# The gates of a small mixture of experts: spread by a matmul, or stored and loaded as broadcast rows

## The reference

```python
def _L3_ffn_ref(x, gate_w, gate_bias, w1, w2, w3, ws1, ws2, ws3):
    scores = jax.nn.sigmoid(xf @ gate_w.T)              # 16 experts
    s = scores + gate_bias
    group_scores = s.reshape(T, 4, 4).max(axis=-1)      # keep 2 of 4 groups
    ...
    _, idx = jax.lax.top_k(s_masked, TOPK)              # 4 experts a token
    comb = zeros(T, E).at[arange(T)[:, None], idx].add(scores at idx)
    h = silu(einsum('td,eid->tei', xf, w1)) * einsum('td,eid->tei', xf, w3)   # 64 hidden an expert
    y = einsum('tei,edi,te->td', h, w2, comb)
    z = silu(xf @ ws1.T) * (xf @ ws3.T) @ ws2.T         # the shared expert, no weight
    return x + y + z
```

## Time and profile before

| | us |
|---|---|
| median of 3 runs | 1003.78 |
| lowest, highest | 1000.64, 1007.53 |
| the profiled execution | 1007.03 |
| its span in the trace | 1005.2 |

### The profile page before, as it was taken

How to read it: one execution, slowest core, us unless ns; L and a number is a source line. 1 busy time by engine, 2 the same in 40 slices (tenths; PEclk the granted TensorE clock), 3 DMA queues, 4 the chain that set the end, 5 groups by cost and what they waited for, 6 DMA issues and landing times. The chain is left out here.

```text
span 1005.2 us, 13391 instructions
## 1 busy us (share of the span) xinstructions
PE 730.2 (73%) x3910; PEld 465.9 (46%) x3910; DVE 590.4 (59%) x2022; ACT 355.2 (35%) x634; POOL 251.8 (25%) x304
## 2 busy tenths in 40 slices
PE   2677762849839775588575757869886688699998
PEld 1233322848838621234364545556654233245554
DVE  6666644326305453775534564979887666576773
ACT  5355420624415332533332311212332466433231
POOL 2240466440343262512423321230210110000000
PEclk9999775869959767977896866989998899799999
DMA  6272022424524330215212100010220120000000
GB/s 175 56 269 74 24 86 69 120 89 116 152 66 130 101 100 19 76 48 204 61 49 80 49 6 1 1 71 2 62 61 17 32 71 25 0 1 11 11 11 11
DMA packets 71218, 65.55 MB, mean 65 GB/s; under 512 B 8996, under 2 KB 62941, under 8 KB 70634
## 3 DMA queue, kind: packets, MB, share of 16 engines
q1 hardware_dynamic: 53610, 48.02, 16.2%
q0 software_dynamic: 5120, 10.50, 3.5%
q10 hardware_dynamic: 12416, 6.16, 2.2%
HBM read 35.61 MB, written 22.94 MB: 58 GB/s over the span
## 5 line engine op out<-in xcount | busy, mean ns | idle before, releaser
L2540 POOL TENSOR_SCALAR s_vare<-s_mv 128x4 f32<-128x4 f32 x40 | 10.9, 272 | 433.8 <-DVE s_mv L1213 422.3
L1326 DVE TENSOR_REDUCE s_nmx<-psum_all 128x4 f32<-128x308 f32 x192 | 83.4, 473 | 56.8 <-PE psum_all L656 54.4
L2097 ACT ACTIVATE s_hT<-psum_all 77x1024 f32<-77x1024 f32 x96 | 96.0, 1017 | 57.2 <-PE psum_all L677 40.3
L675 PE MATMUL psum_all<-s_t,s_ks 128*77 128x512 bf16 x192 | 83.2, 434 | 10.5 <-ACT s_hT L2097 4.8
L656 PE MATMUL psum_all<-s_ks,s_t 128*128 128x308 bf16 x192 | 57.4, 348 | 40.4 <-DVE s_nmx L1326 25.5
L908 PE MATMUL psum_all<-s_arena,s_hT 128*128 x376 | 62.4, 300 | 32.1 <-issue 32.0
L677 PE MATMUL psum_all<-s_t,s_ks 128*77 128x512 bf16 x192 | 82.4, 429 | 0.0
L699 PE MATMUL psum_all<-s_hT,s_v 77*32 77x512 f32 x384 | 59.0, 688 | 32.2 <-ACT s_hT L2097 30.8
L2450 POOL DMA_INDIRECT s_w<-routed_y,s_cT x64 | 61.5, 961 | 69.6 <-issue 69.6
L2436 POOL DMA_INDIRECT routed_x<-s_x_normed,s_cT x64 | 62.5, 977 | 51.4 <-DVE s_cT L1527 33.1
L908 PEld LDWEIGHTS psum_all<-s_arena,s_hT 128*128 128x128 f32 x376 | 55.0, 204 | 36.1 <-issue 35.1
(11 more groups left out here) (311 smaller groups left out, 1555.1 us busy)
## 6 DMA issues: line engine op xcount, KB each, us to landing
s_t<-q_parts SPq DMA_DIRECT2D x66, 128.0 KB, 2.8
routed_y<-s_hT ACTq DMA_DIRECT2D x22, 256.0 KB
s_ks<-s_att SPq DMA_DIRECT2D x72, 77.0 KB, 2.1
q_parts<-s_qparts SPq DMA_DIRECT2D x11, 384.0 KB
s_arena<-in_w SPq DMA_DIRECT2D x2, 2048.0 KB, 10.3
s_h<-routed_x SPq DMA_DIRECT2D x48, 64.0 KB
s_x_normed<-routed_x SPq DMA_DIRECT2D x46, 64.0 KB
routed_x<-s_w SPq DMA_DIRECT2D x34, 64.0 KB
```

The lines of the kernel that those rows point to most:

```text
L675: pe.matmul(PS[0:SK, k + y, :], KS1[:, h, keys], T1[:, u % QS, h // HPG, :], start=True, stop=False)
L1326: read(job, dve.tensor_reduce(nmx[:, u % 2, i, HPG * g:HPG * g + HPG], PS[:, k, 0:HPG * SK].rearrange("p (h s) -> p h s", h=HPG), AX.X, AL ...
L2097: read(("S", L, b, p), nc.scalar.activation(Eexp[:, (PAIRS * u + p) % ES, :, :], PS[0:SK, k:k + 2, :], ACT.Exp))
```

## The change

The combine weights are no longer split and spread by a matmul. C is transposed in float32 (CT), ScalarE copies 16 rows of 512 to cT, and SP stores them to a memory tensor CD[b] (32 KB), waits for that, and loads them back four times 512 KB: each of 16 rows to 64 partitions, two halves of the partitions by two groups of four pairs. The destination, gates, has two buffers per group, by batch parity. VectorE's second multiply reads them; pair 8, whose weight is 1, has a single multiply. New semaphores: s_gated (the multiply done), s_cd, s_gate. The pick_pair load, its copy and the splits are gone; six semaphores of the attention units are shared. The places of layer 7's routing and of (7,0) in layer 6 change.

```diff
     6: {"M0": (0, 0, 0), "M1": (1, 1, 0), "M2": (2, 2, 0), "M3": (3, 3, 0), "MT": (6, 3, 7),
-        "front": (2, 0, 3), "R": (3, 4, 4), "CT": (7, 6, 7), "Q": (2, 2, 3), "stats+": (0, 6, 0),
+        "front": (1, 0, 2), "R": (2, 3, 3), "CT": (6, 0, 7), "Q": (2, 2, 3), "stats+": (0, 6, 0),
-    7: {"front": (1, 1, 3), "R": (1, 3, 3), "CT": (7, 6, 8), "stats": (0, 0, 0), "norm": (0, 2, 0)},
+    7: {"front": (1, 0, 1), "R": (2, 2, 2), "CT": (5, 0, 6), "stats": (0, 0, 0), "norm": (0, 0.9, 0)},
...
# TensorE
-                    have(("CT", L, b))
-                    k = start(("CB", L, b, p), SMALL)
-                    finish(("CB", L, b, p), pe.matmul(PS[:, k, :], pick7[:, 128 * p:128 * p + 128],
-                                                      cT7[:, b % 2, :], start=True, stop=True))
...
-                    have(("CB", L, b, p))
+                    pe.wait_ge(s_gated, GLU_PAIRS * b + p + 1)
# VectorE, glu_unit
+                    if p < GATED:
+                        read(("H", L, b, p), dve.tensor_tensor(gl[:, x, 0, :], PS[:, k + 1, :], gl[:, x, 0, :], ALU.mult))
+                        settled(("H", L, b, p))
+                        if p % 4 == 0:
+                            dve.wait_ge(s_gate[p // 4], 32 * (b + 1))
+                        dve.tensor_tensor(gl[:, x, 1, :], gates[b % 2][p // 4][:, p % 4, :], gl[:, x, 0, :], ALU.mult).then_inc(s_gated, 1)
+                    else:
+                        read(("H", L, b, p), dve.tensor_tensor(gl[:, x, 1, :], PS[:, k + 1, :], gl[:, x, 0, :], ALU.mult))
+                        settled(("H", L, b, p))
+                        dve.sem_inc(s_gated, 1)
# ScalarE, glu_unit
-                        act.wait_ge(*slots.is_read(("CB", L, m // GLU_PAIRS, m % GLU_PAIRS)))
+                        act.wait_ge(s_gated, n - 2)
# SP
-            sp.dma_start(H5[0:64, 0:GLU_PAIRS, :], A["pick_pair"]).then_inc(s_rows, 16)
...
+            def spread_gates(b):
+                if b >= 2:
+                    sp.wait_ge(s_gated, GLU_PAIRS * (b - 1))
+                sp.wait_ge(*slots.is_read(("CT", 7, b)))
+                sp.dma_start(CD[b], cT[0:EXPERTS[7], b % 2, :]).then_inc(s_cd, 16)
+                sp.wait_ge(s_cd, 16 * (b + 1))
+                by_half = CD[b].rearrange("(a p h) c -> a h p c", a=2, h=2)
+                for x in range(2):
+                    if b:
+                        sp.wait_ge(s_gate[x], 32 * b)
+                    for half in range(2):
+                        sp.dma_start(gates[b % 2][x][64 * half:64 * half + 64, :, :],
+                                     by_half[x, half].partition_broadcast(64)).then_inc(s_gate[x], 16)
             for u in range(8, 12):
                 place_q(u)
+            spread_gates(0)
             for b in range(NB):
+                if b + 1 < NB:
+                    spread_gates(b + 1)
                 sp.wait_ge(*slots.is_read(("Y", 7, b)))
                 sp.dma_start(od[:, TPB * b:TPB * b + TPB, :], X[:, TPB * b:TPB * b + TPB, :]).then_inc(s_out, 16)
```

## The result

| | kernel before | changed kernel |
|---|---|---|
| median of 4 runs, us | 1002.21 | 1030.67 |
| lowest, highest | 1000.54, 1007.53 | 1025.79, 1036.10 |
| the profiled execution, its span | 1007.03, 1005.2 | 1025.79, 1024.0 |
| mean granted clock of the span | 0.852 | 0.826 |

The changed kernel is slower: 1.0276 of the time before, 95% interval 1.0238 to 1.0313. The medians differ by 28.5 us where 12.5 were forecast, and 1030.67 is past the end of the range. The direction and the three waits came out as laid out; three sizes in the last layer and the gain ahead of it did not.

A forecast was written before the change was run, and what follows sets the result against it. TensorE was taken to bound the last layer. The terms, -4.2 + (41.6 - 35.8) + 2 x (35.7 + 1.0 - 30.9) - 4.5 - 1.3 + 3 x 1.7 = +12.5, on 1003.78 gave 1016 us; range 996 to 1025.

The forecast's parts named there:

- the three waits: Units (7,0) to (7,2): TensorE waits 2.4 us for the norm, 2.1 for the copy, 4.7 for the routing.
- gates late, (7,1) to (7,3): Reloaded weights reach pair 0's second multiply 0.3 to 1.9 us late, taken as 1.0 in (7,1) and (7,2); (7,3) has room.
- clock, gates late: TensorE's clock falls behind the waits in units that route: 0 to 2.8 us a unit, taken as 1.7.
- (d): Routing of (7,0) inside (6,3) ends sooner, so the last layer starts 3 to 4.5 us earlier, taken as 4.2.
- (a): Last layer: the weight-spreading matmul goes, 36 times; a pair takes 2.62 us, saving 0.51, 18.4 in all.
- (b): VectorE loses one multiply of 0.69 us in nine and five operations per batch; reading the operand from SBUF costs nothing.
- the unit (7,0): Last layer's first unit takes 41.6 us against 35.8, with divide, table load, attn_out and slow clock added.
- (c): At the start, the pick_pair load goes and the first norm comes sooner: 0 to 1.6 us saved, taken as 1.3.
- gates come late by a round trip at half the rate: Rival for the gate loads: 1 MB takes 10 us, 15 us lost in all, 1031 us; chance 0.07.
- The saving stands: Rival: the gain of 24 us comes without added waits, 980 us; range 978 to 998, chance 0.15.
- The balance: Rival: full clock, gates in time and a better (7,0) leave +2, 1006 us; range 998 to 1009, chance 0.23.

The follow-up runs named there:

- e11: Changed kernel with spare matmuls in TensorE's waits and batch 0's gates alone loaded, used for all batches: 1.0127 of the kernel before, last layer 138.75 us.
- e10: Changed kernel with spare matmuls (12, 6, 17) where TensorE waits before pairs 3, 4 and 5: 1.0206 of the kernel before, last layer 145.6 us.
- e9: The changed kernel as it is, run beside e10 and e11 on their chip: 1.0300 of the kernel before, last layer 155.4 us.
- e3: Changed kernel with gates loaded for batch 0 alone and used for all batches, no spare matmuls: 1.0139 of the kernel before, last layer 144.0 us.
- e2: Changed kernel with only layer 7's R and CT places put back wide, norm and copy left early: 1.0057 of the kernel before, last layer 136.5 us.
- e1: Changed kernel with all of layer 7's routing and norm places as wide as before: 0.9943 of the kernel before, last layer 123.1 us.
- e6: e1 with the gates loaded in three groups, pair 0 first: 0.9911 of the kernel before, 993.40 us, last layer 118.85.
- e7: e6 with CT one step later: 0.9896 of the kernel before, 992.89 us, last layer 118.4.
- e8: The kernel before with only the change's layer 6 places for the routing of (7,0): 0.9992 of the kernel before.
- e4: The same kernel as e10, with spare matmuls in TensorE's waits, on another chip: 1.0127 of the kernel before, last layer 144.4 us.

## Why the prediction came out as it did, step by step

| term of the sum, us | forecast | measured | from |
|---|---|---|---|
| the layer at full clock, gates in time (but for (7,0)) | 136.7 | 138.75 | e11 |
| gates late, (7,1) to (7,3) | +2.0 | +6.8 | e10 less e11 |
| clock, gates late | +5.1 | +9.8 | e9 less e10 |
| the layer | 143.8 | 155.4 | e9 |
| less the layer before | 125.9 | 125.9 | |
| (d) the way into the layer | -4.2 | -1.4 | below |
| start, and what is left | -1.3 | +0.4 | 28.5 - 29.5 + 1.4 |
| in all | +12.4 | +28.5 | |

(The forecast's 12.5 is this 12.4 with stages rounded one by one. The last row but one mixes medians with single profiles: the interval of the ratio is 3.7 us either way, and the changed kernel and its variants begin the last layer anywhere from 863.6 to 872.4 on this kind of chip. So that row says little.)

*Right: (a), and the saving per pair.* Without waits a hidden matmul follows its like by 2.61 us; 2.62 was the forecast. e11's last unit takes 23.66, forecast 23.7. *(b)* holds: L1782, with both operands in SBUF, takes 0.69.

*Right: the three waits.* Laid out as 2.4, 2.1 and 4.7; measured 2.27 (e3, gates out of the way), 1.90 and 4.34. At full clock with no gates to wait for, the unit takes 35.56, forecast 35.7. Their cause is the order: e2 takes away the routing's wait and most of the copy's, and e1 the norm's as well. The forecast's own signs of being wrong were a wait of TensorE below 8 us a unit, which did not come, and a wait of VectorE above 2 us for a load of pair 0, which did, just: 1.97, 1.19, 2.04 and 2.12 us in the four units of the changed kernel, and 1.99 to 2.70 at full clock (e10).

The Trainium skill (ScalarE: Activation LUTs, What ACT_TABLE_LOAD costs) had a drain of 1.38 us on top of each load. The trace of the changed kernel shows none: L2135's load starts at 934.20, 1.54 after L2108's at 932.66, with 1.28 for that load and the sigmoid (0.22) between.

*Too small: the unit (7,0).* 41.6 was forecast, with 1.7 of slow clock in it; it takes 43.97 at a clock of 0.96 (e11). TensorE's timeline there has two waits that (7,1) doesn't have in that size:

```profile
873.69 1.13 PE L790 MATMUL psum_all<-s_x_turned,s_arena 128*128 128x512 f32 x2 [1.03 <-DVE s_hT L1788]
...
899.76 1.84 PE L790 MATMUL psum_all<-s_x_turned,s_arena 128*128 128x512 f32 x2 [3.12 <-DVE s_hT L1788]
```

The second is the step with a chunk and the divide, costed at 2.0; it is 2.7 longer than the 0.42 that stands there in (7,1). In the changed kernel itself most of it lies under the lowered clock (0.67 left), so the table's parts are those of one order of taking away. The first I had not laid out: VectorE starts late behind add_out and the table load. What counts more comes behind it. In e11 pair 3 starts 11.75 us into the unit, 8.64 in (7,1). Of these 3.1 us the forecast had 1.28, for the table load; most of the rest is the wait of 1.71 for batch 0's own gates, shown above, for which it had nothing, as it let gates be late in (7,1) and (7,2) only. In e6 and e7, where it is gone, (7,0) takes 34.0 and 32.5. As for the 1.03: in the kernel before only 0.20 of wait was there, with a first pair at half rate above it (1.92), which the new kernel doesn't have; that the one covered the other is argued, not shown.

*Mis-sized: the gates, 6.8 for 2.0.* The failed step is the landing. I took the first megabyte, in 4.6 to 6.2 us, as if it had the DMA engines to itself. All four loads are issued within 2.55 us, as the timeline of SP in the changed kernel shows:

```profile
907.62 0.32 SPq L2679 DMA_DIRECT2D gates<-s_cT  x1
909.20 2.55 SPq L2686 DMA_DIRECT2D s_w<-gates  x4
```

and they share the engines, from 914.02 on with the store of the output as well. The multiply starts at 916.80, 7.6 after the first issue (in e10 904.62 to 913.74, 9.1). The DMA part of the same stretch, 909 to 921 in 40 slices, has all engines busy at some 210 GB/s:

```profile
DMA  0000076999989999999999999999999999999999
GB/s 0 0 0 0 0 123 171 355 328 212 177 184 253 225 246 218 218 212 198 184 205 198 198 253 218 205 205 191 184 212 198 239 218 218 205 198 205 150 190 292
```

At 210 GB/s the first megabyte alone would have taken 5.0 us, my estimate from that rate, which is what the forecast had; it took 7.6 with the second under way beside it. The 10.3 of the earlier trace rows I had misread: it is the median of two landings, 8.1 and 12.6, and over those 13.1 us (64.40 to 77.50 in the kernel before) the engines moved 341 GB/s. The lateness itself, 1.19 and 2.04 us in (7,1) and (7,2) of the changed kernel, is not far from the 1.0 (0.3 to 1.9) that I took; at full clock, where the units are shorter and the gates wanted sooner, it is 2.70 and 2.39. The store was cheaper than I took it (907.62 to 909.20, 1.58 for 2.4). Also wrong was that (7,3) has room: it lost 1.63 between e10 and e11. The Trainium skill's 2 us and bytes over 436 GB/s (DMA: Bandwidth & Descriptors, Anatomy of one DMA) is a fit for single DMAs that GpSimd issues, where these four are issued by SP; the estimate of 4.4 us for the first megabyte from it stands against 7.6 here, and the measurement decides.

*Mis-sized: the clock, 9.8 for 5.1 where the gates are late*, and past my bound of 2.8 a unit: e9's first three units lose 2.9, 4.4 and 2.9 against e10's, the last gains 0.4. I took one stretch behind one wait from the earlier trace rows and let chunks cover it. In the changed kernel (7,1) has two such stretches, behind the copy's wait and the routing's, and (7,0) and (7,2) a third behind the norm's. That they are the cost and not only go with it is what e10 shows: with TensorE given work in its waits, and the norm, the copy and the routing as they were on the other engines, the time returns. With the gates out of the way the clock costs 5.3 (e3 to e11, two chips), as forecast; what was missed may so be the part that the late gates add to it.

*Wrong: (d), 4.2 for 1.4.* From the output matmuls of (6,2) to the layer's start it is 25.6 us in the changed kernel (839.74 to 865.36), 26.8 in e8 and 27.0 before. So the move brings 0.2, and the splits that are gone 1.2. The failed sentence is "later by up to 1.5 where CT holds the last values up": it holds them up by nearly all that was saved. The timelines of VectorE and TensorE in the changed kernel show why:

```profile
852.90 0.71 DVE L1352 STREAM_TRANSPOSE s_att<-s_att 128x512 f32<-128x512 f32 x1
...
860.40 0.22 DVE L1443 TENSOR_TENSOR s_combine<-s_r 128x64 f32<-128x64 f32 x1
...
860.68 1.02 PE L746 MATMUL psum_all<-s_consts,s_combine 128*16 128x128 f32 x4 [4.26 <-DVE s_combine L1443]
```

VectorE's divide (852.90 to 855.60) stands between the first chunk and the rest, so the weights are ready at 860.6 and no sooner. Counted from the output matmuls of (6,2), as above, that is 869.0 on the clock of the earlier trace rows, 1.7 to 2.8 later than the 867.3 or 866.2 that I laid out; I had left the divide out.

*(c), the start:* the first norm stands 3.0 us earlier in the trace (13.47; 16.46 before), but the medians can't show it, as the interval of 3.7 us either way is wider than the term; how much of the 1.3 reached the end was not measured apart and stays open.

*The rivals.* That gates come late by a round trip at half the rate was named with 1031 us, nearly the time measured, but it is not what happened: it had 1 MB take 10 us at half the rate, where it took 7.6 to 9.1 at 210 GB/s shared with the second; its price of 15 us was twice the 6.8, and the clock made up the rest. That its total is near is luck. The saving stands only once the order is mended (e1, e6). The balance counted on full clock and gates in time and had neither.

## What to carry to other kernels

In engines that work their lists in order, a side chain costs next to nothing only while each of its steps is given as much cover by main steps as it is long; moved one step nearer, it stops all that is queued behind it. Count such waits first, then price the stretch behind each as well: here 9.8 us of lowered clock came on top of the waits. A broadcast load wants its first rows as a load of their own, since the loads issued behind it share the engines and it lands with them.

## What was not expected of the hardware

Granted clock: a wait of 1.90 us behind one of 3.23 in (7,1) was followed by hidden matmuls at half rate (2.01 for 1.12, the 1.2 GHz level), and one of 4.34 by the same. Behind the 3.23 alone the pair there still ran at full rate (922.00, 1.12), while behind the same wait in (7,0) and (7,2) it did not (2.08 and 2.07). So units with the same waits differ: 39.6 and 43.8 us for (7,1) and (7,2) in one profile, 42.6 and 40.8 in two others.

Loads that repeat a row of 2 KB over 64 partitions moved some 210 GB/s with all 16 engines busy, where the two large loads of the earlier trace rows had 341.

The same kernel takes 924.5 us on one chip and 1002.0 on another; the last layer of the kernels that ran on both is the same within 1%, so the difference lies ahead of it (in e4 the layer begins at 793.6, in e10 at 863.6). Why was not looked into.
